# Summing a mixture-of-experts result in DRAM by accumulating transfers instead of gathering and adding on the core

## The reference

```python
xn = _layernorm(x, axis=-1)
x = x + _L1_attn_ref(xn, ...) + _L1_ffn_ref(xn, ...)

# _L1_attn_ref returns xn + swiglu(y) @ w_out.T, y a cumulative attention over _rms(xn)
# _L1_ffn_ref, 2048 tokens, 16 experts, two of them for each token:
scores = jax.nn.softmax(logits, axis=-1)
topk_w, topk_idx = jax.lax.top_k(scores, K)
combine = jnp.sum(jax.nn.one_hot(topk_idx, E) * topk_w[..., None], axis=1)
h = _swiglu(jnp.einsum('th,ehj->etj', x, w_gate_up), I)
y = jnp.einsum('eti,eih,te->th', h, w_down, combine)
y = y + _swiglu(x @ shared_gate_up, SI) @ shared_down
```

## Time and profile before

| what | value |
|---|---|
| median of 3 runs | 576.57 us (575.61 to 578.02) |
| the profiled execution's own time | 575.75 us |
| its span, first to last instruction | 573.9 us |
| mean granted TensorE clock | 0.964 |
| busy in the span: PE, DVE, ACT, POOL | 513.9, 391.0, 266.4, 215.2 us |

### The profile page before, as it was taken

How to read it: one execution, slowest core, us unless ns; L and a number is a source line. 1 busy time by engine, 2 the same in 40 slices (tenths; PEclk the granted TensorE clock), 3 DMA queues, 4 the chain that set the end, 5 groups by cost and what they waited for, 6 DMA issues and landing times.

```text
span 573.9 us, 7170 instructions
## 1 busy us (share of the span) xinstructions
PE 513.9 (90%) x2368; PEld 370.6 (65%) x2368; DVE 391.0 (68%) x838; ACT 266.4 (46%) x511; POOL 215.2 (38%) x170
## 2 busy tenths in 40 slices
PE   2889679778997999999998888999999999999991
PEld 1345335654475867777775676877776877877881
DVE  3889999977999679985889997623324323223357
ACT  4466257527663664664885531343332333233220
POOL 0310735240313241425145352225647665564200
PEclk9999989798999899999999997999999999999997
DMA  8700004030032000032457035712223222223167
GB/s 289 308 0 1 1 0 148 5 142 0 1 111 90 22 1 1 1 120 70 153 186 211 16 111 183 218 38 73 74 75 113 89 72 89 88 79 79 37 231 255
DMA packets 24228, 54.25 MB, mean 95 GB/s; under 512 B 3296, under 2 KB 11872, under 8 KB 24192
## 3 DMA queue, kind: packets, MB, share of 16 engines
q1 hardware_dynamic: 19680, 41.46, 21.4%
q0 software_dynamic: 4512, 12.33, 7.2%
HBM read 36.08 MB, written 17.70 MB: 94 GB/s over the span
## 4 chain that ended last, share of the span: by engine, by line
PE 65%; DVE 23%; ACT 4%; issue 3%; DMA 2%; POOL 2%; DVEq 0%; ACTq 0%; POOLq 0%
PE bank L255 47%; PE bank L407 8%; PE bank L323 2%; DVE tk L899 2%; DVE m L897 2%; PE bank L435 2%; PE bank L462 2%; DVE r_bt L1096 2%; DVE fd L960 1%; DVE ff L867 1%; DVE hs L1006 1%; PE bank L296 1%; DVE rw L1129 1%; DVE tk L906 1%; PE bank L312 1%
## 5 line engine op out<-in xcount | busy, mean ns | idle before, releaser
L255 PE MATMUL bank<-fe,w_qkv 128*128 128x512 f32 x192 | 90.8, 606 | 3.5 <-ACT fe L578 1.0
L1109 DVE TENSOR_TENSOR m_h<-m_h,bank 128x176 f32<-128x176 f32 x47 | 15.9, 338 | 89.5 <-ACT m_h L729 89.5
L1237 POOL DMA_INDIRECT y_rows<-m_y,dest x47 | 46.4, 988 | 63.2 <-DMA y_rows<-m_y,dest 40.2
L255 PE MATMUL bank<-mw,m_xt 128*128 x188 | 65.6, 472 | 0.0
L255 PEld LDWEIGHTS bank<-fe,w_qkv 128*128 128x128 f32 x192 | 36.0, 195 | 42.4 <-issue 38.0
L1228 POOL DMA_INDIRECT xg<-xn_rows,tab x47 | 46.2, 982 | 38.4 <-DVE second L1103 16.4
L255 PE MATMUL bank<-yhr,wsg_h 128*128 128x512 f32 x128 | 58.4, 456 | 0.8 <-DVE hs L1006 0.8
L255 PE MATMUL bank<-yhr,wsg_l 128*128 128x512 f32 x128 | 50.6, 396 | 0.0
L255 PE MATMUL bank<-hyr,wsg_h 128*128 128x512 f32 x128 | 50.6, 395 | 0.0
L255 PE MATMUL bank<-mw,m_ht 88*128 x188 | 48.4, 379 | 0.0
L255 PEld LDWEIGHTS bank<-mw,m_ht 88*128 88x128 f32 x188 | 35.3, 189 | 11.3 <-issue 0.6
(11 more groups left out here) (207 smaller groups left out, 1255.2 us busy)
## 6 DMA issues: line engine op xcount, KB each, us to landing
mw<-in_gu SPq DMA_DIRECT2D x16, 352.0 KB
ga<-y_rows SPq DMA_DIRECT2D x8, 512.0 KB, 8.5
mw<-in_dn SPq DMA_DIRECT2D x16, 176.0 KB
fa<-in_x SPq DMA_DIRECT2D x4, 512.0 KB, 3.9
stage<-in_wsg SPq DMA_DIRECT2D x4, 512.0 KB, 13.0
spilled_x<-fa SPq DMA_DIRECT2D x4, 512.0 KB, 2.8
hx<-spilled_x SPq DMA_DIRECT2D x4, 512.0 KB, 3.8
spilled_r<-fb SPq DMA_DIRECT2D x4, 512.0 KB, 4.9
```

Of the source, the lines that this page charges most:

```text
L255: mm = e.matmul(o, a, b, start=n == 0, stop=n == len(terms) - 1)
L1109: e.tensor_tensor(m_h[j % 3][:, :], m_h[j % 3][:, :], ps("ju", j)[:, 176:352], ALU.mult).then_inc(s["jh"], 1)
L1237: e.indirect_dma_start(out=y_d, out_offset=bass.IndirectOffsetOnAxis(ap=dest[:, j:j + 1], axis=0), in_=m_y[j % 3][:, :], in_offset=None).t ...
```

## The change

The output tensor gets 128 spare rows ahead of the 2048 real ones, and everything is added up in it:

* `rspill(b)` stores the residual rows straight into the output. `rback`, `park`, `unpark`, `yload`, `combine` and `store` go, with their tensors.
* `routed` now also carries the weight of each slot: each one-hot row is multiplied by three values (token number, weight rounded, rest of the weight), so its matmuls are 144 columns wide for 48 or 96. `onehot` has two buffers for three. `table()` gives the weight of each slot (gslot); an unused slot gets a spare row of its own, the same in xn_rows and in the output.
* `jout(j)` multiplies by gslot as it copies. `yput(j)` scatters into the output and adds to what is there.
* `dout(b, i)` is a copy on ScalarE from the bank to rw. `dadd(b)`, new, is a transfer of 512 KB issued by GpSimd that adds rw to the rows of batch b in the output.
* Every adding transfer waits for the one before it, `yput` and `dadd` alike (`adding()`), and the first of them for all four `rspill` and for the spare rows.
* The lists of all engines are new.

```diff
             def routed(g, *n):
-                twice = 1 if g < 4 else 2
                 for k in range(4):
-                    mm = e.matmul(o[:, 0:twice * TW].rearrange("p (z j) -> p z j", j=TW), r_bt[g % 3][:, k * P:(k + 1) * P],
-                                  r_at[g % 3][:, None, k * TW:(k + 1) * TW].broadcast_to([P, twice, TW]),
+                    mm = e.matmul(o[:, 0:3 * TW], r_bt[g % 2][:, k * P:(k + 1) * P], r_at[g % 2][:, 3 * TW * k:3 * TW * (k + 1)],
                                   start=g == 0 and k == 0, stop=False, skip_group_check=True)
...
+            def dout(b, i):
+                if b > 1:
+                    q.wait_ge(d_add, 16 * (b - 1))
...
+                q.wait_ge(s["dw"], CHUNKS * (b + 1))
+                e.activation(RW[b % 2][:, i, :], ps("acc", b, i)[:, :], ACT.Copy).then_inc(s["od"], 1)
...
             def jout(j):
                 if j > 2:
                     q.wait_ge(d_my, 16 * (j - 2))
+                q.wait_ge(s["rt"], 30)
                 q.wait_ge(s["jd"], j + 1)
-                e.tensor_copy(m_y[j % 3][:, :], ps("jd", j)[:, 0:D]).then_inc(s["jy"], 1)
...
+                e.tensor_scalar(m_y[j % 3][:, :], ps("jd", j)[:, 0:D], gslot[:, j:j + 1], None, ALU.mult).then_inc(s["jy"], 1)
...
+            added = []
+
+            def adding():
+                if added:
+                    q.wait_ge(*added[-1])
+                else:
+                    for m in d_rs:
+                        q.wait_ge(m, nth(NB - 1))
+                    q.wait_ge(d_pad, 32)
+
             def yput(j):
-                q.wait_ge(s["rt"], 29)
-                if j:
-
-                    q.wait_ge(d_my, 16 * j)
                 q.wait_ge(s["jy"], j + 1)
-                e.indirect_dma_start(out=y_d, out_offset=bass.IndirectOffsetOnAxis(ap=dest[:, j:j + 1], axis=0),
-                                     in_=m_y[j % 3][:, :], in_offset=None).then_inc(d_my, 16)
+                adding()
+                e.indirect_dma_start(out=out, out_offset=bass.IndirectOffsetOnAxis(ap=tab[:, j:j + 1], axis=0),
+                                     in_=m_y[j % 3][:, :], in_offset=None, compute_op=ALU.add).then_inc(d_my, 16)
+                added.append((d_my, 16 * (j + 1)))
+
+            def dadd(b):
+                q.wait_ge(s["od"], 2 * b + 2)
+                adding()
+                e.dma_start(out[P + b * T:P + (b + 1) * T, :].rearrange("(i p) d -> p i d", p=P), rows_[b % 2], accum_op=ALU.add).then_inc(d_add, 16)
+                added.append((d_add, 16 * (b + 1)))
...
             def rspill(b):
                 q.wait_ge(s["res"], b + 1)
-                e.dma_start(rs_d[b], FB[b % 2].rearrange("p h n -> p (h n)")).then_inc(d_rs[b % 2], 16)
+                e.dma_start(out[P + b * T:P + (b + 1) * T, :].rearrange("(i p) d -> p i d", p=P), FBr[b % 2]).then_inc(d_rs[b % 2], 16)
```

The lists on TensorE, near the end, one line of each:

```diff
-            dup(3, 6, 0); xdown(45, 1); dgate(3, 7, 3); xdown(46, 2); dup(3, 7, 4); ddown(3, 5, 6, 7); ddown(3, 6, 6, 7); dgate(3, 8, 0); dup(3, 8, 1)
+            hturn(46, 5); dgate(3, 10, 0); xdown(45, 3); ddown(3, 8, 6, 7); dup(3, 10, 1); xdown(46, 4); ddown(3, 9, 6, 7); ddown(3, 10, 6, 7)
```

More of the change, by code:

```diff
@@ L176, in build @@
         slot_i, eoff = tile("slot_i", 32, U32), tile("eoff", TW, U32)
-        tab, dest, second = tile("tab", TW, U32), tile("dest", TW, U32), tile("second", TW)
+        tab, gslot, spare, val = tile("tab", TW, U32), tile("gslot", TW), tile("spare", TW), tile("val", 96, F32R)
         m_y = [also(f"m_y{n}", top_at + 2560 + 256 * n, D) for n in range(2)] + [also("m_y2", E * EW, D)]
@@ L478, in tensor @@
[L478 to L481, removed]
@@ L494, in tensor @@
[L494 to L497, removed]
@@ L498, in tensor @@
[L498 to L501, removed]
@@ new lines, in tensor @@
+            dup(2, 5, 1); ddown(2, 3, 6, 7); routed(6); dgate(2, 6, 4); dup(2, 6, 2); ddown(2, 4, 6, 7); dgate(2, 7, 0); routed(7); dup(2, 7, 5)
+            ddown(2, 5, 6, 7); dgate(2, 8, 1); dup(2, 8, 4); ddown(2, 6, 6, 7); xturn(0, 2); dgate(2, 9, 3); xturn(1, 0); xup(0, 5); ddown(2, 7, 6, 7)
+            xturn(2, 2); dup(2, 9, 1); hturn(0, 4); xup(1, 0); dgate(2, 10, 2); xturn(3, 5); hturn(1, 4); xup(2, 3); xdown(0, 1); xturn(4, 0)
+            hturn(2, 4); xup(3, 5); xdown(1, 3); xturn(5, 4); hturn(3, 1); xup(4, 0); ddown(2, 8, 6, 7); xdown(2, 5); xturn(6, 3); hturn(4, 1)
@@ new lines, in tensor @@
+            xup(5, 4); xdown(3, 0); xturn(7, 5); hturn(5, 1); xup(6, 3); xdown(4, 2); xturn(8, 4); dup(2, 10, 0); hturn(6, 1); xup(7, 5); xdown(5, 3)
+            xturn(9, 2); hturn(7, 4); xup(8, 5); dgate(3, 0, 1); xdown(6, 2); xturn(10, 5); hturn(8, 4); xup(9, 3); xdown(7, 0); xturn(11, 2)
+            hturn(9, 4); xup(10, 5); ddown(2, 9, 6, 7); xdown(8, 3); xturn(12, 5); hturn(10, 0); xup(11, 1); xdown(9, 2); xturn(13, 4); hturn(11, 0)
+            xup(12, 5); xdown(10, 1); xturn(14, 3); hturn(12, 0); xup(13, 2); dup(3, 0, 4); xdown(11, 5); xturn(15, 1); hturn(13, 0); xup(14, 3)
@@ new lines, in tensor @@
+            xdown(12, 2); xturn(16, 5); hturn(14, 0); xup(15, 4); xdown(13, 1); ddown(2, 10, 6, 7); xturn(17, 3); hturn(15, 5); xup(16, 4); xdown(14, 2)
+            dgate(3, 1, 1); xturn(18, 0); hturn(16, 5); xup(17, 4); xdown(15, 3); xturn(19, 2); dup(3, 1, 0); hturn(17, 4); xup(18, 3)
+            ddown(3, 0, 6, 7); xdown(16, 2); xturn(20, 5); hturn(18, 3); dgate(3, 2, 1); xup(19, 4); xdown(17, 2); xturn(21, 0); dup(3, 2, 5)
+            hturn(19, 4); xup(20, 2); dgate(3, 3, 0); xdown(18, 3); xturn(22, 4); hturn(20, 2); xup(21, 1); xdown(19, 5); xturn(23, 3); hturn(21, 4)
@@ new lines, in tensor @@
+            xup(22, 2); xdown(20, 1); xturn(24, 3); hturn(22, 4); xup(23, 2); xdown(21, 5); xturn(25, 3); hturn(23, 1); xup(24, 4); xdown(22, 2)
+            ddown(3, 1, 6, 7); xturn(26, 3); hturn(24, 4); xup(25, 1); dup(3, 3, 5); xdown(23, 4); xturn(27, 3); hturn(25, 1); xup(26, 0); xdown(24, 2)
+            xturn(28, 3); dgate(3, 4, 1); hturn(26, 0); xup(27, 4); xdown(25, 3); dup(3, 4, 2); xturn(29, 0); hturn(27, 5); xup(28, 4); xdown(26, 0)
+            ddown(3, 2, 6, 7); xturn(30, 5); hturn(28, 4); xup(29, 3); xdown(27, 0); xturn(31, 5); hturn(29, 4); xup(30, 3); xdown(28, 1); xturn(32, 0)
@@ new lines, in tensor @@
+            ddown(3, 3, 6, 7); hturn(30, 5); xup(31, 4); xdown(29, 2); xturn(33, 3); hturn(31, 1); xup(32, 5); dgate(3, 5, 0); xdown(30, 4)
+            xturn(34, 2); hturn(32, 1); xup(33, 3); xdown(31, 5); dup(3, 5, 0); xturn(35, 4); hturn(33, 2); xup(34, 1); xdown(32, 3); dgate(3, 6, 5)
+            xturn(36, 0); hturn(34, 4); xup(35, 1); xdown(33, 3); xturn(37, 0); hturn(35, 2); xup(36, 4); ddown(3, 4, 6, 7); xdown(34, 1); dup(3, 6, 3)
+            ddown(3, 5, 6, 7); xturn(38, 2); hturn(36, 0); xup(37, 4); xdown(35, 2); dgate(3, 7, 5); xturn(39, 0); hturn(37, 3); xup(38, 1)
@@ L526, in scalar @@
+            dgate(3, 10, 0); xdown(45, 3); ddown(3, 8, 6, 7); dup(3, 10, 1); xdown(46, 4); ddown(3, 9, 6, 7); ddown(3, 10, 6, 7)
         @block.scalar
```

392 lines of the change are left out of this document (175 added, 217 removed).

## The result

| what | before | after |
|---|---|---|
| median of 4 runs each, measured together | 577.21 us | 629.38 us (628.95 to 632.14) |
| ratio | | 1.092, 95% interval 1.088 to 1.096 |
| the profiled execution, and its span | 575.75, 573.9 us | 628.96, 627.1 us |
| mean granted TensorE clock | 0.964 | 0.936 |

The change costs 52 us. The page of the changed kernel first: busy time and instructions of each engine, then slices of 15.7 us, then the transfers that GpSimd issues.

The account below looks back on a forecast made before the run. TensorE was taken to set the pace, with the scatter chain just inside its limit at no cost. From 575.75 us, tail -3.5, last wait -0.4 and routing +1.0 gave 572.9 us; range 567 to 600.

Parts of the forecast that it names:

- The bound: From tile 0 on, the one-by-one scatter chain decides; forecast to end 3 us ahead of TensorE, so costing 0.
- P: Time per adding scatter in the chain: 3.3 us taken, between 2.7 and 5.4; up to 3.37 free.
- its own sum: Chain from tile 0: 12.2 to the first scatter, 5.5 for batch 2's addition, 47 P; limit 175.9 us.
- the signs named for being wrong: jout waiting tens of us for scatters, GpSimd issue well over 1 us, or several us stalled at the first addition.
- the first rival: Scatter chain becomes the bound, GpSimd waiting for each adding scatter: 583.9 us at P 3.6, 598 at 3.9; chance 0.32.
- the second: Each addition is read, added and written in sequence: P 4.2 to 5.4, 612 to 668 us; chance 0.09.
- The padding: Unused slots keep their 0.7 us price despite spare rows: P 3.5, 579 us; counted with the first rival.
- The tail: After TensorE's last matmul: copies 1.3, adding transfer 5.5, end 0.4, so 7.2 us for 10.7: -3.5 us.
- TensorE's last wait: Low part for the last ddown no longer stands behind three combinations on VectorE: -0.4 us.
- Routing: All 32 routing matmuls have 144 columns: between 1.0 and 3.3 us more, +1.0 taken.
- The first addition: On GpSimd it waits for all batches' stored residuals; covered by later dgate and dup, otherwise 2 to 5 us.
- The front: First 370 us, with 11 us of dense work moved ahead of xturn(0): no term, only plus or minus 4 us.

Follow-up runs that it names:

- plain scatters: Changed kernel with yput overwriting the output rows instead of adding to them; 574.23 us, ratio 0.996 to the kernel before.
- two chains: Changed kernel with odd tiles adding into a second tensor under their own semaphore, the two never summed; 570.70 us, ratio 0.987 to the kernel before.

## Why the prediction was wrong, by its steps

**The bound: right, and the limit on P nearly so.** The text named the scatter chain as what decides, with P up to 3.37 us free and 4.7 us lost for each 0.1 above. Put the measured distance into its own sum: at P = 4.6 it ends 12.2 + 5.5 + 216.2 = 233.9 us after the start of tile 0, 58.0 late. With 4.8 more at the end and 7.5 less in front (both below), 572.9 + 58.0 + 4.8 - 7.5 = 628.2, for 628.96 measured. That it comes within 1 us is partly luck, as two errors of 7 us cancel. The chain took 241.3 us from tile 0 to the last addition's start (375.1 to 616.40), not 233.9: 13.4 to the first scatter, 6.8 for batch 2's addition, and 47 turns of 4.7 in the mean, since some are longer than 4.6 (397.73 to 403.48, beside a fetch of 512 KB that SyncE issued at 400.48). And the 572.9 carries 6.6 us of TensorE's time beyond the prices of its work (6.0 that it took in the kernel before, 0.6 from the terms for routing and the last wait), which a chain of scatters does not bear. The limit itself was set a little high: with plain scatters 3.19 apart TensorE took 184 us from tile 0 on (377.5 to 561.6) and was busy in 178.8 of them, with two chains 178.4 (377.5 to 555.9) and busy in 177.8, so a P just under the limit already costs 5 to 6 us.

**The step that failed is the size of P**, 3.3 taken and 4.55 to 4.6 measured. I built it from below: a plain scatter, 2.7, and two corrections of 0.3, both for the transfer itself. The measured turn has three more parts than a plain one, and two of them I had put at nothing. The runs show 2.7 + 0.6 + 0.7 + 0.5 = 4.5:

* The issue, put at nothing. An adding scatter takes GpSimd 0.6 us longer (0.99 to 1.59). "More descriptors may lengthen the issue" stood in the rival; I gave it no price.
* The transfer, 0.6 taken. From start to landing it is 3.8 us, not 2.5; 0.6 of this is the issue, 0.7 the rest. So this part was nearly right in its sum, though not by its row: the 451 GB/s of the earlier trace rows are those of a plain gather and a plain scatter, whose bytes pass in 0.5 us. Those of one adding scatter take 1.3 us, 11 of the 40 slices of this window (602.0 to 606.6 us), and in 144 packets, where a plain one has 48 on average (4512 over 94, gathers among them):

```profile
GB/s 0 0 0 0 0 0 0 0 0 0 0 0 0 0 0 0 0 0 0 0 0 0 0 0 0 0 0 62 71 36 62 36 62 178 178 223 125 107 0 0
```

* The order of the waits, put at nothing: 0.5 us a turn and 20 us in all. It stood in the diff, which I quoted, and I read it as nothing.

Two of the signs named for being wrong came with it: `jout` waits 54.2 us for scatters, and an issue is well over 1 us.

The Trainium skill, page "Collectives: The Full Stack", section "The bandwidth ceiling", says of a ring's ReduceScatter that the adding in the transfer engine costs no time and that reading two sources halves the rate. The trace comes near it: the best rate of the dense rows fell from 355 to 207 GB/s. By that alone P would have been 3.0; the issue and the order of the waits, which no such rate contains, made most of the rest.

**The rivals.** What happened is the mechanism of the first rival, 0.32, at the size of the second: "P from 4.2 to 5.4, 612 to 668", 0.09. The second one's name was not borne out, for nothing shows a reading, adding and writing in sequence, but a bound of 5.4 stood in the prediction, and the range stopped at 600. The cost is steep, 47 us for each microsecond of P, so the value taken near the lower bound deserved less trust than it got. The padding did not keep its price.

**The tail: wrong, in the other direction than its sign.** The copies and hand-over are 1.5 us for 1.3 (561.56 to 563.04 with plain scatters). The adding transfer and the end are 10.5 us for 5.9: 6.3 or 6.4 to land for the last one (5.5 said) and over 4 of nothing (0.4 said). So even without the chain the new tail, 12.0 us, would be longer than the old one, 10.7: the term is +1.3 instead of -3.5. The 0.4 came from a store of SyncE; the transfer that ends the changed kernel is GpSimd's. By the fit of the Trainium skill, page "DMA: Bandwidth & Descriptors", section "Anatomy of one DMA", an estimate of the landing is 3.2 us, or 4.4 with the second read. The plain transfer of GpSimd agrees with the first (last byte after 2.9 us); for the adding one both are too low, 5.9 to 6.4 measured.

**TensorE's last wait: right.** The low part starts at 606.75, 0.03 us after its input; it was 0.44. **Routing: not told apart.** The 32 matmuls have a median of 0.28 us at 144 columns; all that waits for them is VectorE, once and 0.4 us. **The first addition: right.** GpSimd waited 1.02 us for the stored residuals. **The front: outside its margin.** By the start of `xturn(0)` before, 371.4, and 11.2 us more work ahead, it would be 382.6; it is 375.1, and 377.5 in two other kernels with these lists, so 5 to 7.5 us better, for plus or minus 4.

**A lower clock is part of the picture, not a cause.** From 375 us to its end TensorE was busy 197.6 us, for the 177.8 with two chains. With two chains it had hardly a gap and a granted clock of 1.00, as in the kernel before from 371 to 563. Here the clock is 1.00 from 375 to 420, then 0.89, 0.94 and 0.93 in stretches of 50 us in which it was idle for 7 to 11 us, and 0.82 from 570 to 609. 1.00 is the level of 2.4 GHz; the lower figures are means over it and the level of 1.2 GHz. Since TensorE waits for the chain in these stretches, the slower matmuls hardly add to the time; no run changed the clock alone.

## What to carry to other kernels

Where accumulating transfers into shared rows are taken one by one, as in this kernel, cost them as a latency times a count, the latency from one start through issue, data and hand-over to the next start, and compare that with the time per item of the engine that feeds it; a reading at the lower bound is no estimate. Work on the core that is largely hidden (32 combinations, many of them in the shadow of TensorE) is cheap to keep, and a transfer that replaces it is not free because no engine is busy. Where two waits precede a transfer of GpSimd, put the one that will come last in front of the one that is long met (20 us here), and look which queue the program's very last transfer is on.

## What the runs showed that I had not expected

* The order of two waits ahead of GpSimd's transfer is worth 0.48 us each time: 0.75 against 0.27 us from landing to the next start (609.3 against 629.4 us for the kernel).
* The addition costs GpSimd 0.6 us of issue, for 128 rows of 1 KB (0.99 to 1.59) and for 512 KB (0.83 to 1.43) alike.
* 512 KB with addition go at 207 GB/s at best in 528 packets, without at 355 GB/s in 144 from GpSimd and at 354 GB/s in 528 from SyncE.
* After GpSimd's transfer as the last one, adding or not, 4 to 5 us pass without a record before the span ends; after SyncE's store 0.4 in one kernel and 1.7 in another.
* A VectorE operation of 0.69 us lasted 2.82 while GpSimd ran adds of 128x1024, in one place of one run.
